# Attention: the eight value matmuls of a pair of units are issued in two parts, four in the odd unit and four in the even unit that follows

## What is computed

```
q, k, v = x @ Wq + bq, x @ Wk + bk, x @ Wv + bv      # B=8, S=512, D=512, 16 heads of 32
scores = einsum('bhqd,bhkd->bhqk', q / sqrt(32), k) + attention_bias
scores = where(src_mask, -inf, scores)
probs = softmax(scores, axis=-1)
ctx = einsum('bhqk,bhkd->bhqd', probs, v)
x = x + (ctx @ Wo + bo)
```

## Time and profile before

| | |
|---|---|
| median of 3 runs | 3154.49 us (3151.41 to 3159.67) |
| the profiled execution, its own time | 3153.09 us |
| its span | 3151.4 us |
| TensorE's mean granted clock over the span | 0.957 of full |
| PE busy (matmuls) | 2801.7 us, 89% |
| PEld busy (weight loads) | 2262.7 us, 72% |
| DVE busy | 1898.9 us, 60% |
| ACT busy | 1121.8 us, 36% |
| POOL busy | 1032.6 us, 33% |

### The profile page before, as it was taken

One profiled execution on the slowest core, in us unless ns is written; L12 is line 12 of the kernel. 1 busy time (PEld: TensorE's weight loads), 2 busy tenths in 40 slices (PEclk: granted clock), 3 DMA queues, 4 the chain that ended last, 5 costly groups with the idle time before them and its releaser, 6 DMA issues. The chain is left out here.

```text
span 3151.4 us, 45864 instructions
## 1 busy us (share of the span) xinstructions
PE 2801.7 (89%) x14049; PEld 2262.7 (72%) x14065; DVE 1898.9 (60%) x3706; ACT 1121.8 (36%) x2255; POOL 1032.6 (33%) x752
## 2 busy tenths in 40 slices
PE   6965999999999999969999999997898988988986
PEld 3424788888888888857877778776676766766764
DVE  8945777777787777755434443433664555555543
ACT  1115777777776777711111111111111111111111
POOL 1005667665666757532000001001331221222110
PEclk9987999999999999989999999998999999999997
DMA  4325676767667676631000000001432332232310
GB/s 162 105 92 150 194 204 180 206 180 206 195 184 207 182 202 186 183 92 61 27 27 28 27 13 15 27 14 49 151 124 90 97 108 90 94 110 91 103 31 34
DMA packets 255618, 356.47 MB, mean 113 GB/s; under 512 B 26570, under 2 KB 113610, under 8 KB 252682
## 3 DMA queue, kind: packets, MB, share of 16 engines
q1 hardware_dynamic: 253610, 350.20, 37.3%
q0 software_dynamic: 1760, 3.19, 0.4%
HBM read 268.91 MB, written 34.05 MB: 96 GB/s over the span
## 5 line engine op out<-in xcount | busy, mean ns | idle before, releaser
L819 POOL TENSOR_TENSOR at_bias<-at_bias,at_mask 128x1024 f32<-128x1024 f32 x224 | 481.0, 2150 | 366.5 <-DMA at_bias<-in_fside_Bx16xSxS 364.7
L1218 DVE TENSOR_TENSOR at_pL<-at_bank_probT,at_pH 128x512 fp32r<-128x512 f32 x512 | 351.1, 686 | 207.7 <-ACT at_pH L930 205.9
L923 ACT ACTIVATE at_y<-at_bias,at_nmax 128x512 f32<-128x512 f32 x512 | 368.3, 719 | 58.1 <-DVE at_nmax L1212 56.8
L930 ACT ACTIVATE at_pH<-at_bank_probT 128x512 fp32r<-128x512 f32 x512 | 304.6, 595 | 205.8 <-PE at_bank_probT L1073 200.9
L1212 DVE CUSTOM_DVE_ANT_0 at_bias<-at_bias,at_bank_score 128x512 f32<-128x512 f32 x512 | 346.1, 676 | 4.0 <-ACT at_y L923 1.5
L1589 POOL TENSOR_SCALAR expert_WH<-expert_stage 128x1024 fp32r<-128x1024 f32 x128 | 154.3, 1206 | 583.7 <-PE expert_bank_out L98 458.9
L1073 PE MATMUL at_bank_probT<-at_ident,at_y 128*128 128x128 f32 x2048 | 311.3, 275 | 37.2 <-DVE at_pL L1218 29.8
L1906 DVE CAST ff_gH<-ff_g 128x512 fp32r<-128x512 f32 x128 | 68.0, 531 | 425.9 <-ACT ff_g L1662 425.9
L1662 ACT ACTIVATE ff_g<-ff_bank_hid,ff_b1c 128x512 f32<-128x512 f32 x128 | 88.3, 690 | 646.3 <-PE ff_bank_hid L98 646.3
L1662 ACT ACTIVATE expert_g<-expert_bank_hid,expert_b1c 128x512 f32<-128x512 f32 x128 | 88.3, 690 | 644.3 <-PE expert_bank_hid L98 638.8
L1073 PEld LDWEIGHTS at_bank_probT<-at_ident,at_y 128*128 128x128 f32 x2048 | 246.3, 141 | 97.8 <-issue 28.1
(11 more groups left out here) (311 smaller groups left out, 6326.5 us busy)
## 6 DMA issues: line engine op xcount, KB each, us to landing
at_bias<-in_fside_Bx16xSxS SPq DMA_DIRECT2D x256, 512.0 KB, 4.6
expert_stage<-in_L_cond_Wi SPq DMA_DIRECT2D x128, 256.0 KB, 2.7
expert_stage<-in_L_cond_Wo SPq DMA_DIRECT2D x128, 256.0 KB, 2.8
at_q<-at_nat SPq DMA_DIRECT2D x384, 64.0 KB, 3.5
at_k<-at_nat SPq DMA_DIRECT2D x384, 64.0 KB, 2.9
st_f<-in_x SPq DMA_DIRECT2D x8, 1024.0 KB, 7.3
x_after_layer<-st_y SPq DMA_DIRECT2D x8, 1024.0 KB, 4.8
at_x<-x_after_layer SPq DMA_DIRECT2D x32, 256.0 KB, 4.1
```

Source lines behind the costliest of these rows:

```text
L819: pool.tensor_tensor(bias[i % NB][:, :, :], bias[i % NB][:, :, :], mask[:, 2 * i % R:2 * i % R + 2, :], ALU.add).then_inc(s_bm, 1)
L923: act.activation(prob[u % 2][:, :], bias[u // 2 % NB][:, u % 2, :], ACT.Exp, scale=-1.0, bias=nmax[:, u % 4:u % 4 + 1], accum_out=sums[:, ...
L930: act.activation(pH[u // 2 % 2][:, :, u % 2, :], pT[u % 2][:, :].rearrange("p (k q) -> p k q", q=P), ACT.Copy).then_inc(s_pth, 1)
L1218: dve.tensor_tensor(pL[u // 2 % 2][:, :, u % 2, :], pT[u % 2][:, :].rearrange("p (k q) -> p k q", q=P), f32(pH[u // 2 % 2][:, :, u % 2, :] ...
```

## The change

`values` gets a third argument, `part`. Part 0 (four matmuls, key blocks 0 and 1) stays in the odd unit u = 2p + 3 with all of the waits; part 1 (key blocks 2 and 3) goes to the even unit u = 2p + 4, behind its transposes and score matmul, and raises `s_pv`. The copies and additions of the context whose pair now ends in the same unit as they stood in go one unit later, on ScalarE from 2, 18, 34, 50 to 3, 19, 35, 51, on VectorE from 3, 19, 35, 51 to 4, 20, 36, 52.

```diff
-            low_at = {2: -1, 14: 0, 18: 1, 30: 2, 34: 3, 46: 4, 50: 5, 62: 6}
+            low_at = {3: -1, 14: 0, 19: 1, 30: 2, 35: 3, 46: 4, 51: 5, 62: 6}
...
-                    if u in low_at and (prev or u > 2) and (cur or u == 2):
+                    if u in low_at and (prev or u > 3) and (cur or u == 3):
                         copy_low(n, low_at[u])
...
-            def values(n, p):
+            def values(n, p, part):
...
-                pe.wait_ge(s_ptl, n * NU + 2 * p + 2)
-                if p % 8 == 0:
-                    pe.wait_ge(s_vl, n * C + c + 1)
-                if p % 4 == 0 and not (is_first(n) and t < 2):
-                    pe.wait_ge(s_add, n * NT + t - 1)
-                for k in range(4):
-                    for part, probs in enumerate((pH, pL)):
+                if part == 0:
+                    pe.wait_ge(s_ptl, n * NU + 2 * p + 2)
+                    if p % 8 == 0:
+                        pe.wait_ge(s_vl, n * C + c + 1)
+                    if p % 4 == 0 and not (is_first(n) and t < 2):
+                        pe.wait_ge(s_add, n * NT + t - 1)
+                for k in (2 * part, 2 * part + 1):
+                    for low, probs in enumerate((pH, pL)):
                         mm = pe.matmul(pC[t % 2][:, half * 2 * P:(half + 1) * 2 * P],
                                        v[c % 2][:, k * 2 + t % 2, 3 * g:3 * g + 4, :].rearrange("p b d -> p (b d)"), probs[p % 2][:, k],
-                                       start=(p % 4 == 0 and k == 0 and part == 0), stop=(p % 4 == 3 and k == 3 and part == 1))
-                mm.then_inc(s_pv, 1)
+                                       start=(p % 4 == 0 and k == 0 and low == 0), stop=(p % 4 == 3 and k == 3 and low == 1))
+                if part == 1:
+                    mm.then_inc(s_pv, 1)
...
                     if u % 2 == 1 and (prev or u > 1) and (cur or u == 1):
-                        values(n, (u - 3) // 2)
+                        values(n, (u - 3) // 2, 0)
+                    if u % 2 == 0 and (prev or u > 2) and (cur or u < 3):
+                        values(n, (u - 4) // 2, 1)
...
-            high_at = {3: -1, 15: 0, 19: 1, 31: 2, 35: 3, 47: 4, 51: 5, 63: 6}
+            high_at = {4: -1, 15: 0, 20: 1, 31: 2, 36: 3, 47: 4, 52: 5, 63: 6}
```

More of the change, by code:

```diff
@@ L1279, in body @@
                         invert(n, c - 1)
-                    if u in high_at and (prev or u > 3) and (cur or u == 3):
+                    if u in high_at and (prev or u > 4) and (cur or u == 4):
                         add_high(n, high_at[u])
```

## The result

The changed kernel takes 3175.96 us in the median of 4 runs (3174.15 to 3177.23); the kernel before takes 3153.57 in the same comparison (4 runs, 3151.41 to 3159.67). The ratio is 1.0067 (1.005 to 1.0085): 22.4 us slower, where 13.4 had been worked out. Sign and mechanism were right, the size was too small. The profiled execution took 3176.72 us with a span of 3174.9, 23.5 more than before.

What follows compares the result with a forecast made beforehand. TensorE was taken to bound the kernel, busy 862.82 of 900 us. Terms 7.8 + 1.9 + 0.5 + 1.5 + 1.0 + 0.7 = 13.4 us on 3153.09 gave 3166.5, forecast as 3167, range 3152 to 3176.

Steps and rivals of the forecast that it cites:

- Bound and chain: TensorE sets the pace; where it stands still, the chain is ScalarE's high-half copy H, VectorE's low-half subtraction L, transposes T.
- The new wait, 1.42 us from T(even) to H(even): Even units: the high-half copy waits for the moved matmuls, 1.42 us behind the transposes instead of 0.71, so 0.24 later.
- Units 25 to 33, 7.8 us: Largest term: T(33) 1.06 us later in six batches, 0.71 in the second and last; sum 7.8 us.
- the list of signs: Closing list of what the trace would show, among it H(28) 0.5 us later against T(27) than before.
- The hold: Unit 28 in six batches: transposes held, then a restart, making H(28) and T(32) 0.59 us later; least trusted.
- TensorE's busy and idle time: In the attention stage: TensorE's busy time unchanged, its idle time up by 7 to 13 us.
- Start of batch, 0.37 each: T(1) 0.52 us late, less 0.15 for no restart: five batches 1.9 us; two behind a loop branch 0.5 us.
- Units 42 to 51, 1.5 us: H(42) moves by 0.17 us, carried to T(50); T(51) 0.37 late, 0.22 without a restart; seven batches 1.5 us.
- Unit 7, 1.0 us: T(7) held through H(4), L(4), L(5): all eight batches would give 1.9 us, half taken, 1.0 us.
- The moved copies, zero: Context copies and additions at units 2/3, 18/19, 34/35, 50/51 going one unit later were to cost zero.
- the end of the last batch: Paced by ScalarE and VectorE, no projections left: new wait costs 0 to 1.7 us, 0.7 taken.
- The rival of absorption: Unit 61's wait for keys absorbs the delay: 0 to +8 us, 3159 if DMAs land independently; chance 0.26.

Runs made afterwards that it cites:

- copies: The kernel before with only the context's moved copies and additions (units 3, 19, 35, 51 on ScalarE, 4, 20, 36, 52 on VectorE): 3152.41 us, ratio 0.998.
- the two kernels without the key wait: The changed kernel and the kernel before, each with the DMAs stacking the next batch's queries and keys issued one unit earlier: ratios 1.0028 and 0.9983.

## Why the prediction was right, and where it was short

*Bound and chain.* Right. TensorE sets the pace, and the loss lies where it stands still or has just done so. With the second half ahead of T(even) the ratio is 0.9983, and with three buffers, which take the wait away, 1.0016.

*The new wait, 1.42 us from T(even) to H(even).* 1.35 in the fifth batch where TensorE is not held, 1.52 where it is, as at T(28) after a restart.

*Units 25 to 33, 7.8 us.* 9.0, and 6.6 without the clock. The share of T(27) was 0.15 to 0.17 in six batches and 0.3 in two, where 0.24 was expected. In the restart at T(28) I had taken L(26) to stay 1.46 behind T(27); it is earlier against it (1.26), so H(28) is 0.10 later against T(27) and not 0.35 (the list of signs said 0.5, which doesn't follow from the sum). T(28) itself starts 2.08 behind T(27), almost as soon as TensorE is ready, and is hardly held. T(32) to T(33) grew by 0.50 as said. The hold, in which I trusted least, was the term that I oversized. The second batch, which I had set apart for having no hold at T(28), differs by half clock: T(28) is 3.51 behind T(27) there, 2.49 to 2.51 in the others.

*TensorE's busy and idle time.* Wrong. From the first batch's T(0) to the last one's T(63) its busy time rose by 17.3 us (1011.5 to 1028.8), where no change was forecast, and its idle time by 5.4 instead of 7 to 13. Half clock, where the same matmuls have longer rows, is a part of it and not all: the kernel before in its second profile, with six such stretches, has 1017.4, and the changed kernel with earlier stacks, with two, has 1022.0. Another part are waits too short to leave a gap between the rows. T(26) of the fifth batch with the last value matmul ahead of it and the score product behind it, before and after:

```profile
877.94 0.28 PE L1088 MATMUL at_bank_ctx<-at_pL,at_v 128*128 128x256 f32 x1
878.06 0.60 PE L1073 MATMUL at_bank_probT<-at_ident,at_y 128*128 128x128 f32 x4
878.42 0.48 PE L1065 MATMUL at_bank_score<-at_k,at_q 96*128 96x512 f32 x1
```

```profile
890.59 0.28 PE L1089 MATMUL at_bank_ctx<-at_pL,at_v 128*128 128x256 f32 x1
890.87 0.63 PE L1073 MATMUL at_bank_probT<-at_ident,at_y 128*128 128x128 f32 x4
891.39 0.50 PE L1065 MATMUL at_bank_score<-at_k,at_q 96*128 96x512 f32 x1
```

T(26) starts 0.28 behind the matmul instead of 0.12, and the product 0.52 behind T(26) instead of 0.36: 0.3 us that the list of waits doesn't have and the busy time counts. How the rise divides between the two was not separated.

*Start of batch, 0.37 each.* 0.22 to 0.42 in five batches, 0.88 and 0.59 at the two loop branches, which both have half clock there. T(1) of the fifth batch starts straight behind TensorE's last product, as said, 2.81 behind T(0).

*Units 42 to 51, 1.5 us.* In the fifth batch T(51) is 0.31 later against T(41), near the 0.22, but 0.18 of it is gone by T(53). In all batches together 0.8 is left from T(33) to T(53). Why the rest is given back I did not separate.

*Unit 7, 1.0 us.* 1.55: the wait reaches T(7) in every batch with 0.15 or more, not in half of them.

*The moved copies, zero.* Right but for the end of the last batch, where they cost 1.1 of the 1.65; in the "copies" kernel that stretch lost the same without the new wait.

*The step that fell short* is not in this list: in the sum I gave unit 61 and the clock nothing, and no reason for it. The rival of absorption, in which the new delays "shrink to what exceeds 1.2 us a batch" if the DMAs land at a time of their own, does not hold: the keys follow the exponentials (T(53) to the issue 7.04 and 7.03), as I had held against it, so nothing is absorbed. In the first pair of profiles 9.2 us were lost in unit 61, 4.8 of them later keys and 4.4 half clock. The missing terms are the issue of the query stacks and the half clock behind the halts. How much of them is the change's is not shown, as the 5.3 us against the second profile of the kernel before tell. The order was sized about right: 11.0 in the sum for the places where four profiles show 9.9 to 11.7. The 14 us between the two kernels without the key wait, against 13.4, agree with that within a wide interval. That the sum fits is in part luck: its four terms were 7.8, 1.5, 1.0 and 0.7, and the places measured 6.6, 0.8, 1.55 and 1.65, so they miss by 0.55 to 1.2 us in both directions.

*What stays open.* Why SyncE takes 3.68 us for six DMAs in one batch and 5.35 in another. Whether the change makes the long issue and the half clock likelier, or only meets them: two profiles of the changed kernel have eight stretches, the one with 24 more transposes four, the two of the kernel before one and six. Against a simple link with the order speaks the kernel with eight matmuls behind the even score product: its issue takes 3.68 or 3.69 us in all seven batches, and it has four stretches. More than that no run tells.

*The rule weighed.* By the share of weight loads, 83%, the displaced matmuls would have found room and the time stayed near 3154. In "Perfetto Trace Analysis", section "Identifying the Most-Contended Engine", the Trainium skill puts this share above matmul busy time as a measure; by it the ratio would be near 1.0. It was 1.0067, and even without unit 61's wait 1.0045. For short matmuls at 0.12 us from start to start the spacing of the starts was the better guide.

*The clock.* The rows show two levels, and a halt of the same length followed by either (2.25 and 2.26 us in unit 61; 1.76 before T(27) in the second and the fourth batch before the change). "TensorE: Matmul & The Clock Gate", section "What's actually happening", of the Trainium skill says that the clock follows how busy the engine has been, and that this isn't aligned to when a kernel starts, so that the same kernel can meet it differently. The traces agree with this: one stretch and six in two profiles of the same program.

## What to carry to other kernels

Moving work behind an instruction that is itself held doesn't fill the halt; it lengthens what comes after it, and a semaphore raised by the last of the moved pieces makes the next engine late as well. Put such work ahead of the held instruction: the same split then costs nothing. Where an engine halts for a microsecond or two again and again, read the granted clock stretch by stretch too, since a halt can cost its own length and half clock behind it; and profile the unaltered kernel twice before a difference of 5 us at one place is explained.

## What was not expected of the hardware

- After a halt of 1.6 to 2.6 us TensorE sometimes ran at the lower clock level and sometimes did not. Behind the halt before T(27) it cost 1.2 us (14.05 against 12.87), in unit 61 1.5 (6.79 against 5.26).
- The issue of six DMAs on SyncE's queue took 3.68 to 5.35 us in the first two profiles, and 5.53 in one batch of the changed kernel's second. In the fifth batch after the change one of the six took 1.17 and the median 0.59:

```profile
L684 SPq DMA_DIRECT2D at_q<-at_nat x6: 513/590/1173, 953.7 to 957.4; - x6
```
